# First expert stage: product A11·B11 leads, A12·B21 in front of the first down products, and the roundings of weights in front of the first silu

## The reference, cut to what matters

```python
def _L0_cond_ref(hidden_states, gating_probs, shared_gate_prob, Wg, Wu, Wd, Sg, Su, Sd):
    E, B, S, D, F = (8, 2, 256, 256, 1024)
    g = jnp.einsum('bsd,edf->ebsf', h, Wg)
    u = jnp.einsum('bsd,edf->ebsf', h, Wu)
    expert_outs = jnp.einsum('ebsf,efd->ebsd', jax.nn.silu(g) * u, Wd)
    expert_output = jnp.einsum('be,ebsd->bsd', gating_probs, expert_outs)
    shared = jnp.einsum('bsf,fd->bsd', jax.nn.silu(h @ Sg) * (h @ Su), Sd)
    sg = shared_gate_prob[:, :, None]
    return (1.0 - sg) * expert_output + sg * shared
```

## Time and profile before

| what | us |
| --- | --- |
| median of 3 runs | 2124.18 (2120.98 to 2127.06) |
| the profiled execution's own time | 2124.22 |
| its span in the trace | 2122.4 |
| PE busy | 1920.0 (90% of the span) |
| DVE, ACT, POOL busy | 1482.5, 1115.6, 899.0 |
| first matmul of the stage's products to the last | 21.9 to 1145.3 |

### The profile page before, as it was taken

How to read it: one execution, slowest core, us unless ns; L and a number is a source line. 1 busy time by engine, 2 the same in 40 slices (tenths; PEclk the granted TensorE clock), 3 DMA queues, 4 the chain that set the end, 5 groups by cost and what they waited for, 6 DMA issues and landing times. The chain is left out here.

```text
span 2122.4 us, 35240 instructions
## 1 busy us (share of the span) xinstructions
PE 1920.0 (90%) x12206; PEld 1611.6 (76%) x12206; DVE 1482.5 (70%) x2400; ACT 1115.6 (53%) x2117; POOL 899.0 (42%) x858
## 2 busy tenths in 40 slices
PE   5999999999999999999998677999899766959998
PEld 4778878787887878788787555788799645849998
DVE  6777777767777776777776896433588575857776
ACT  4555554545555454555544597232355364636664
POOL 5442251504224150422400085220388234968885
PEclk9999999999999999999999789999999887979999
DMA  4101010010101001010101301310256114556661
GB/s 151 60 1 60 1 59 0 0 59 0 59 0 59 0 0 59 0 59 0 28 1 51 69 3 35 127 42 8 70 193 198 57 27 129 187 184 206 211 214 55
DMA packets 96322, 144.51 MB, mean 68 GB/s; under 512 B 15358, under 2 KB 72608, under 8 KB 96096
## 3 DMA queue, kind: packets, MB, share of 16 engines
q1 hardware_dynamic: 89168, 127.21, 18.6%
q0 software_dynamic: 4928, 12.86, 1.7%
q10 hardware_dynamic: 2128, 3.15, 0.4%
HBM read 111.46 MB, written 14.16 MB: 59 GB/s over the span
## 5 line engine op out<-in xcount | busy, mean ns | idle before, releaser
L314 PE MATMUL ps<-cond_x_lo,cond_w_hi 128*128 128x512 f32 x1008 | 394.5, 391 | 0.0
L406 ACT ACTIVATE cond_h_hi<-cond_h 128x512 fp32r<-128x512 f32 x288 | 177.2, 629 | 267.6 <-DVE cond_h L559 267.6
L564 DVE TENSOR_TENSOR cond_h_lo<-cond_h,cond_h_hi 128x512 fp32r<-128x512 f32 x288 | 261.9, 938 | 4.1 <-ACT cond_h_hi L406 0.3
L330 PE MATMUL ps<-cond_h_hi,cond_d_hi 128*128 128x512 f32 x576 | 228.2, 396 | 24.3 <-DVE cond_h_lo L564 23.6
L660 POOL TENSOR_TENSOR cond_w_lo<-cond_stage_up,cond_w_hi 128x512 fp32r<-128x512 f32 x36 | 57.6, 1599 | 439.2 <-ACT cond_w_hi L406 439.2
L314 PE MATMUL ps<-cond_x_hi_first,cond_w_hi 128*128 128x512 f32 x576 | 226.3, 393 | 9.5 <-POOL cond_w_lo L678 7.9
L314 PE MATMUL ps<-cond_x_hi_first,cond_w_lo 128*128 128x512 f32 x576 | 225.3, 391 | 0.0
L330 PE MATMUL ps<-cond_h_lo,cond_d_hi 128*128 128x512 f32 x576 | 224.5, 390 | 0.0
L450 ACT ACTIVATE cond_h<-ps 128x512 f32<-128x512 f32 x216 | 121.5, 596 | 196.0 <-DVE cond_h_lo L564 152.0
L330 PE MATMUL ps<-cond_h_hi,cond_d_lo 128*128 128x512 f32 x576 | 224.4, 390 | 0.0
L542 DVE TENSOR_TENSOR ps<-cond_p_row,ps 128x512 f32<-128x512 f32 x144 | 99.8, 693 | 176.0 <-PE ps L314 176.0
(11 more groups left out here) (408 smaller groups left out, 5182.5 us busy)
## 6 DMA issues: line engine op xcount, KB each, us to landing
moe_stage_up<-in_L_ffn_expert_wv SPq DMA_DIRECT2D x22, 1024.0 KB, 8.8
typed_stage_up<-in_L_cond_wi SPq DMA_DIRECT2D x11, 1024.0 KB, 5.0
typed_stage_dn<-in_L_cond_wo SPq DMA_DIRECT2D x11, 1024.0 KB, 5.5
moe_stage_dn<-in_L_ffn_expert_proj SPq DMA_DIRECT2D x11, 1024.0 KB, 5.3
cond_stage_up<-in_L_cond_Wg SPq DMA_DIRECT2D x7, 1024.0 KB, 5.1
cond_stage_up<-in_L_cond_Wu SPq DMA_DIRECT2D x7, 1024.0 KB, 7.2
cond_stage_dn<-in_L_cond_Wd SPq DMA_DIRECT2D x7, 1024.0 KB, 9.5
rope_v_now<-rope_v_blk SPq DMA_DIRECT2D x16, 272.0 KB, 2.4
```

Of the source, the lines that this page charges most:

```text
L314: ins = pe.matmul(bank, ws[:, j, u, w], xs.rearrange("p o n -> p (o n)"), start=(opens and k == 0), stop=(k == 2), skip_group_check=True)
L330: ins = pe.matmul(y_ps[side][d], w[:, 2 * j + r, d * P:(d + 1) * P], xs[:, tile], start=(j == 0 and r == 0 and k == 0), stop=(j == J - 1 a ...
L406: copy = lambda dst, src: act.activation(dst, src, ACT.Copy)
L564: dve.tensor_tensor(h_lo[:, tile], h[:, tile], h_hi[:, tile], ALU.subtract).then_inc(h_ready, 1)
```

## The change

On PE, A11·B11 goes in front of S1·T1, with a wait of its own (`silu_done` 4g + 1, or `h_made` 4(g − 1) + 1); and A12·B21, with its wait for `p1_kept`, goes in front of `between(0)`, which is d0. Everything behind d0 stands where it stood. On ACT, `keep` copies `bank_a` first and `bank_d` second, and `tasks` goes from behind `keep(e, c, 1)` to behind the roundings of quadrants 11 and 21, in front of the wait for `h_ready` and the first silu. The first wait of the first step asks for two x_lo instead of one. DVE and POOL have the same code.

```diff
                     if start and u == 0:
-                        pe.wait_ge(x_lo_dve, 1)
+                        pe.wait_ge(x_lo_dve, 2)
...
+                    if u == 1:
+                        pe.wait_ge(silu_done, 4 * g + 1)
+                    elif not start:
+                        pe.wait_ge(h_made, 4 * (g - 1) + 1)
+                    product(bank_a, e, c, u, A11, B11, True, p1_done)
                     if u == 1:
                         pe.wait_ge(silu_done, 4 * g + 2)
...
                     product(bank_d, e, c, u, S1, T1, True, p5_done)
                     if start and u == 0:
-                        pe.wait_ge(x_lo_dve, 2)
-                    product(bank_a, e, c, u, A11, B11, True, p1_done)
-                    if start and u == 0:
                         pe.wait_ge(x_lo_dve, 3)
...
-                    between(0)
                     pe.wait_ge(p1_kept, q + 1)
                     product(bank_a, e, c, u, A12, B21, False, p2_done)
+                    between(0)
...
+                    act.wait_ge(p1_done, q + 1)
+                    if not (isinstance(q, int) and q == 0):
+                        act.wait_ge(u2_made, q)
+                    copy(p1_row[:], bank_a).then_inc(p1_kept, 1)
                     act.wait_ge(p5_done, q + 1)
...
                     copy(p5_row[:], bank_d).then_inc(p5_kept, 1)
-                    act.wait_ge(p1_done, q + 1)
-                    if not (isinstance(q, int) and q == 0):
-                        act.wait_ge(u2_made, q)
-                    copy(p1_row[:], bank_a).then_inc(p1_kept, 1)
...
                             round_hidden(pe_e, pe_c, 21, 4)
+                        tasks(e, c, first, last, sums, raws)
+                        if not (first and c == 0):
                             act.wait_ge(h_ready, 4 * g)
...
-                        tasks(e, c, first, last, sums, raws)
```

## The result

The changed kernel takes **2129.35 us** in the median of 15 runs (2127.74 to 2131.02), beside 2123.53 us (2120.98 to 2127.06, 15 runs) for the kernel before: a ratio of 1.0026, with a 95% interval of 1.0019 to 1.0032. It is slower by 5.8 us. The interval excludes 1, so the slowdown is real, but it is within the 0.3% (6.4 us) that the prediction took as its bound. The time lies inside the range of 2108 to 2150; the forecast was 13.1 us slower.

The account below looks back on a forecast made before the run. It took PE's waits in front of `down` (28.5 us) as the bound. Removing 26.4 us of holes and adding 39.5 us, mostly at A22·T4, gave net +13.1 on 2124.2: 2137 us, range 2108 to 2150.

Parts of the forecast that it names:

- The mechanism: POOL roundings and DVE splits working out of SBUF exclude each other; moving POOL's releaser moves which operations meet.
- The holes at d0: PE waits in front of `down` at c = 6, 7, 0, 1, claimed to go wholly: 3.3 us per expert.
- ACT's cover of the silus: With `tasks` in front, the first silu ends at 6.1 us, needed at 7.48: cover 1.4 us, cost 0.
- Part 2: On PE and ACT, A11·B11 first and the copies of `keep` exchanged: claimed cost 0, no gain.
- part 1: On PE, A12·B21 in front of d0: claimed gain 0.05 to 0.2 us per late step.
- The step that failed: Line 678 of POOL asks 0.09 us before split 21 and holds it, delaying A22·T4 at steps with `sums`.
- one extra register row on ACT: Between the rounding of 21 and of the sums; could eat the 0.09 us, but one stood there before too.
- 32 holes of 1.16 us: PE waits at A22·T4 for `lower_right` at c = 6, 7, 0, 1: 1.16 us per step, eight sets of four.
- rival B: Some of the 32 POOL and DVE races go each way, by step: between 2098 and 2137 us, chance 0.08.

Follow-up runs that it names:

- Parts 1 and 2 alone: The changed kernel with `tasks` put back behind `keep(e, c, 1)`, so only the orders of products and kept rows are new: 2122.67 us.
- 384 columns: The changed kernel with the second kept row copied for 384 of 512 columns at c = 0 of the loop over experts 1 to 7: 2136.14 us.
- the run with waits on POOL: The changed kernel with POOL waiting at c = 5, 6, 7, 0, 1 for all four splits of the step before, in front of `tasks`: 2101.94 us.
- The halves: The changed kernel with line 681 of POOL split into two operations of 128 x 512 instead of one of 128 x 1024: 2103.06 us.
- parts 1 to 3 alone: The changed kernel itself, with nothing added, against the kernel before: 2129.35 us, ratio 1.0026.
- part 3 alone: The kernel before with only `tasks` moved in front of the first silu, old orders of products and kept rows: 2138.73 us.
- part 2 undone: The changed kernel with S1·T1 leading again and the copies of `keep` in their old order: 2166.84 us.
- 448 columns: The changed kernel with the second kept row copied for 448 of 512 columns at c = 0 of the loop over experts 1 to 7: 2136.22 us.
- the small operation on ACT: The changed kernel with a 128 x 1 copy on ACT in front of `tasks` at c = 6, 7, 0 and 1: 2098.62 us.
- the down weights rounded first: The changed kernel with `sums` rounding the down weights before the two sums, from c = 5 of the first expert on: 2099.24 us.

## Why the prediction was partly wrong

**The mechanism held.** The holes at d0 go wholly, and a hole in front of A22·T4 takes their place, at 25 steps with `sums`, with the forecast's times to 0.04 us, and at c = 5 with 0.1 us. Parts 1 and 2 alone gain 0.07 us per late step by the traces, within the 0.05 to 0.2 that was given. ACT's cover of the silus was enough: no wait on a silu stands in the list between 94 and 1080 us. Part 2 cost nothing as part of the whole, and undoing it alone costs about 38 us (2166.84 and 2129.35, each against its own runs of before), because the copy of `bank_a` then ends too late for A12·B21. The prediction did not say that part 1 needs it.

**The step that failed** is the lead of 0.09 us, put together from c = 4 and c = 7 of expert 4 and applied to all 32 steps, so that the sum has 32 holes of 1.16 us where 25 came. The text named what could eat it, one extra register row on ACT between the rounding of 21 and of the sums, and set it aside because before there is one in front of the same rounding as well. That row was indeed harmless. The one that mattered stands further up, between the two kept rows, and only at c = 0 of the loop; part 2 put it there. In the old order it is in front of the first copy, and the second starts on time. Seven races went to DVE: 40.0 us of lost time with all 32 holes (the run with 384 columns), 32.5 in the changed kernel. That is 7.5 us, and between the forecast of +13.1 and the +5.8 that came lie 7.3. It was rival B of the prediction, with its price: 2137.3 less 7 x 1.2 is 2128.9, and 2129.35 was measured. I had given B a chance of 0.08, and a result within 0.3% of no change 0.05; a margin of 0.09 us in one sample of a step should have asked for a look at every kind of step, the loop's first one above all.

**The rest of the sum.** The prediction put the first expert and all behind the stage at nothing. They came to -1.6 and +1.1 us between the two profiles, and that they nearly cancel is luck. In the first expert c = 2 loses 3.1 instead of 4.8 us. There the granted clock was lower in the profile of before (columns: us, busy of PE, PEld, DVE, ACT and POOL, granted clock, DMA share, GB/s; first before, then after):

```profile
63.00:67.00 4.00, 4.00 (x12) 3.15 (x11) 2.66 (x3) 1.09 (x2) 3.95 (x4) 0.57 0.00 0
```

```profile
63.00:67.00 4.00, 3.70 (x17) 2.73 (x16) 3.37 (x4) 1.15 (x4) 4.00 (x4) 1.00 0.00 0
```

A mean of 0.57 is 3.4 of the 4 us at the lower of the two levels, 1.2 GHz, and 12 matmuls instead of 17 started in it. PE had been busy for 1.27 of the 3 us ahead in before, and for 1.06 in after, where the clock stayed. Of the twelve kernels' profiles only those of before and of the run with waits on POOL have the stretch; nothing that I changed explains it, and its cause is open. The 1.1 us behind the stage are of the size by which that part differs between runs (977.1 us in the profile of before, 978.2 in that of after, 981.0 in the run with waits on POOL).

**The pair of ports.** The Trainium skill, SBUF — State Buffer, section "SBUF: two separate sides", says that between a DVE operation with two inputs in SBUF and a GpSimd operation that reads SBUF the shared pair of ports goes for the whole instruction to whichever starts first. The races agree from 0.05 us of lead on: split 21 is held for all of line 681. The halves agree with "for the whole instruction". At -0.004 to 0.005 us the start in the trace does not tell who got the pair: rows with POOL 0.002 us ahead show DVE unhindered. The page says nothing of which request wins when an engine's next operation starts while its own last one still holds the pair; in these runs the other engine won it whenever it had asked 0.048 us or more before.

## What to carry to other kernels

Where two engines hold each other up at SBUF as here, the order of two requests can decide and not the amount of work: 0.1 us more of work on ACT in front of POOL's release made this kernel 31 us faster, and less work on ACT made it 7 us slower. So look at the margin of such a race in every kind of step, the first step of a loop above all, where register operations stand, and don't leave one at a tenth of a microsecond: reorder two operations so that it is half a microsecond, or split the long operation, which bounds what a lost race costs. A change that exchanges one hole for another is worth building on when the new hole has a cheap cure: parts 1 to 3 alone were 0.3% slower, and with two roundings exchanged the kernel is 1.2% faster than before.

## What the runs showed of the hardware

In the profiled executions, one of each kernel, a race for the port repeats itself: 25 and 7 of 32 in the changed kernel and in the one with halves, 32 of 32 for POOL in four others (part 3 alone, part 2 undone, 384 and 448 columns) and 32 of 32 for DVE with the small operation on ACT and with the down weights rounded first; at no lead did some go one way and some the other. POOL won with 0.048 us of lead and lost with 0.005. A split of DVE that is held ends 0.54 to 0.55 us after the POOL operation in front of it, with 128 x 1024 and with 128 x 512 alike (c = 6 of after: 624.20 and 623.65; halves: 625.55 and 625.00), and it gets in ahead of a POOL operation that has asked behind the first (the second half, at 624.96). A register operation of 0.046 us between two ACT copies moved the second by 0.09 us where that one followed at once (1.65 instead of 1.56 us into the step), and that was worth 7.5 us of 2129. In front of the first copy it moved nothing behind the second.
